# A two-layer attention kernel: the theta and phi copies move from SyncE's queue to ScalarE's, as four transfers in one slot

## The reference

```python
# layer 0, d = 64
t = W_theta x + b_theta; p = W_phi x + b_phi      # (n, 64, 1024)
f = softmax(t^T p / sqrt(64))                     # (n, 1024, 1024)
x = x + W_fuse (x f^T) + b_fuse
# layer 1
h = group_norm(x, 32 groups) * gn_w + gn_b
q, k, v = W_q h + b_q, W_k h + b_k, W_v h + b_v   # (n, 128, 1024)
a = softmax(q^T k / sqrt(128))
y = x + W_p (v a^T) + b_p
```

## Time and profile before

| | |
|---|---|
| median of the runs | 1922.38 us (1917.98 to 1924.8, 3 runs) |
| the profiled execution | 1909.72 us, span 1907.9 us |
| granted TensorE clock, mean | 0.978 |
| DMA engines' mean share | 81.3% |
| DMAs per kernel | 384 transposes, 256 copies from `tp_hl`, 128 + 128 for `rden`, 32 images in, 64 halves out |

### The profile page before, as it was taken

One profiled execution on the slowest core, in us unless ns is written; L12 is line 12 of the kernel. 1 busy time (PEld: TensorE's weight loads), 2 busy tenths in 40 slices (PEclk: granted clock), 3 DMA queues, 4 the chain that ended last, 5 costly groups with the idle time before them and its releaser, 6 DMA issues.

```text
span 1907.9 us, 34651 instructions
## 1 busy us (share of the span) xinstructions
PE 1715.2 (90%) x8970; PEld 1127.0 (59%) x8970; DVE 1359.3 (71%) x1541; ACT 1409.7 (74%) x2088; POOL 1381.1 (72%) x1449
## 2 busy tenths in 40 slices
PE   4698989999999999999989999999999999999986
PEld 3465655665656665665655655665656666655653
DVE  4577777777777777777777777777777777777764
ACT  3577777778777777877777877777877777877764
POOL 3567776778777778777778777678777778877754
PEclk9999999999999999999999999999999999999999
DMA  4688888888888888888887878888878988878874
GB/s 94 127 160 169 165 174 166 182 178 171 171 176 180 178 181 167 170 170 177 180 182 166 172 169 181 174 175 172 173 170 172 187 180 168 170 168 184 167 145 94
DMA packets 879542, 319.90 MB, mean 168 GB/s; under 512 B 825376, under 2 KB 826272, under 8 KB 879520
## 3 DMA queue, kind: packets, MB, share of 16 engines
q1 hardware_dynamic: 879520, 319.65, 81.3%
HBM read 50.86 MB, written 17.04 MB: 36 GB/s over the span
## 4 chain that ended last, share of the span: by engine, by line
PE 44%; SPq 20%; issue 12%; DMA 8%; POOL 5%; ACT 5%; DVE 4%; POOLq 0%; ACTq 0%; DVEq 0%
PE o_ps L448 17%; PE s_ps L448 16%; SPq L364 10%; PE m_ps L448 6%; DMA theta<-tp_hl 6%; PE s_ps L487 5%; SPq L426 2%; SPq L424 2%; SPq L427 2%; SPq L425 2%; DVE neg_max L750 2%; DMA rden_dram<-rden 1%; POOL k_lo L892 1%; DVE pair L767 1%; ACT e L649 1%
## 5 line engine op out<-in xcount | busy, mean ns | idle before, releaser
L750 DVE TENSOR_REDUCE neg_max<-s_ps 128x1 f32<-128x1024 f32 x512 | 625.5, 1222 | 233.3 <-PE s_ps L448 232.7
L448 PE MATMUL o_ps<-et,v_hi 128*128 128x512 f16 x2048 | 702.7, 385 | 57.5 <-issue 31.2
L448 PE MATMUL s_ps<-phi,theta 128*128 128x512 f32 x1024 | 334.5, 450 | 95.2 <-DMA theta<-tp_hl 86.2
L448 PE MATMUL o_ps<-et,v_lo 128*128 128x512 f16 x1024 | 393.4, 384 | 0.0
L448 PEld LDWEIGHTS o_ps<-et,v_hi 128*128 128x128 f16 x2048 | 204.8, 100 | 303.0 <-issue 98.2
L767 DVE SCALAR_TENSOR_TENSOR pair<-s_ps,pair 128x1024 f16<-128x1024 f32 x256 | 311.2, 1216 | 16.8 <-ACT pair L674 16.8
L649 ACT ACTIVATE s_ps<-s_ps,neg_max 128x1024 f32<-128x1024 f32 x256 | 277.3, 1083 | 58.9 <-DVE neg_max L750 58.3
L448 PEld LDWEIGHTS s_ps<-phi,theta 128*128 128x128 f32 x1024 | 197.2, 196 | 167.6 <-issue 102.4
L892 POOL TENSOR_TENSOR pair<-e_copied,pair 128x1024 f16<-128x1024 f32 x128 | 273.8, 2139 | 22.5 <-ACT pair L672 22.5
L761 DVE SCALAR_TENSOR_TENSOR et<-s_ps,et 128x1024 f16<-128x1024 f32 x128 | 156.8, 1225 | 175.4 <-ACT et L659 175.4
L674 ACT ACTIVATE pair<-s_ps 128x1024 f16<-128x1024 f32 x256 | 261.9, 1023 | 17.5
(11 more groups left out here) (130 smaller groups left out, 2873.0 us busy)
## 6 DMA issues: line engine op xcount, KB each, us to landing
phi<-tp_hl SPq DMA_DIRECT2D x128, 256.0 KB, 3.8
rden_row<-rden_dram SPq DMA_DIRECT2D x128, 256.0 KB, 3.8
xs<-in_x SPq DMA_DIRECT2D x32, 512.0 KB, 4.0
theta<-tp_hl SPq DMA_DIRECT2D x128, 128.0 KB, 3.8
out_y<-y_sb SPq DMA_DIRECT2D x64, 256.0 KB, 2.4
et<-pair SPq DMA_TRANSPOSE x384, 4.6
rden_dram<-rden SPq DMA_DIRECT2D x128, 2.0 KB, 2.1
w_f<-in_w_fuse_t SPq DMA_DIRECT2D x1, 64.0 KB, 2.3
```

Of the source, the lines that this page charges most:

```text
L448: mm = pe.matmul(out, lhs_t, rhs, start=start and n == 0, stop=stop and n == len(terms) - 1)
L750: nc.vector.tensor_reduce(neg_max[:, t % 4:t % 4 + 1], s_ps[:, part(t), :], AX.X, ALU.max, negate=True).then_inc(s_max, 1)
```

## The change

The copies leave SyncE. `tp_hl0` and `tp_hl1` become one tile `tp_hl` of two parts by 1024 pixels. ScalarE issues four transfers in slot 13, each for both halves, after `pair_hi` of tile 12 and after the wait for GpSimd's split of `tp1`. The reciprocals, on VectorE and on SyncE, are made, written and read back one slot earlier (`REC_LAG` = 5 in place of 6). The transpose of tile 12's pair is issued in slot 14; before, it was issued in slot 15 behind the one of tile 13. For the other copied tiles the slot stays.

```diff
+REC_LAG = 5
 LO_SLOTS = {0: 2, 4: 7, 8: 10, 12: 14}
+COPIED_OUT_SLOTS = {0: 3, 4: 8, 8: 11, 12: 14}
...
-TP_COPY_SLOTS = {12: "tp0", 14: "tp1"}
+TP_COPY_SLOT = 13
...
-        tp_hl = [sb(f"tp_hl{n}", [C, 2, HALF], F32R) for n in range(2)]
+        tp_hl = sb("tp_hl", [C, 2, N], F32R)
...
-                for t in [t for t in LO_SLOTS if LO_SLOTS[t] == s - 1]:
+                for t in [t for t in COPIED_OUT_SLOTS if COPIED_OUT_SLOTS[t] == s]:
                     move(it, t, copied_at, s_copied)
...
             def reciprocals_out(it, s):
-                first = s - 6
+                first = s - REC_LAG
...
             def reciprocals_in(it, s):
-                first = s - 7
+                first = s - REC_LAG - 1
...
-            def tp_copies(it, s):
-                unit = next((u for u, name in UNITS.items() if name == TP_COPY_SLOTS.get(s)), None)
...
-                    tp_copies(it, s)
...
+            def tp_copies(it, s):
+                if s != TP_COPY_SLOT or not here(mx_at, it, MX_SLOT):
+                    return
+                act.wait_ge(s_split, before(staged_at, it, s))
+
+                act.wait_ge(s_scores, before(tile_at, it, PHASE))
+                theta_hl, phi_hl = (tp_hl[rows, :, :].bitcast(F32) for rows in (slice(0, D), slice(D, C)))
+                act.dma_start(phi2[0:D, :, :].bitcast(F32), phi_hl).then_inc(s_tp_copy, 16)
+                act.dma_start(phi2[D:C, :, :].bitcast(F32), phi_hl).then_inc(s_tp_copy, 16)
+                act.dma_start(theta2[0:D, :].bitcast(F32), theta_hl[:, 0, :]).then_inc(s_tp_copy, 16)
+                act.dma_start(theta2[D:C, :].bitcast(F32), theta_hl[:, 1, :]).then_inc(s_tp_copy, 16)
...
                     inputs_hi(it, s)
+                    tp_copies(it, s)
...
             def reciprocals(it, s):
-                first = s - 6
+                first = s - REC_LAG
```

More of the change, by code:

```diff
@@ L59 @@
 X_MAX_SLOT = 7
+MX_SLOT = 9
 X_SLOT = 8
@@ L312, in attention_pair @@
         s_den = sem("den_scaled_ready")
-        s_tp_copy = [sem(f"theta_phi_copied{n}") for n in range(2)]
+        s_tp_copy = sem("theta_phi_copied")
         s_split_hi = sem("unit_split_hi")
@@ L463, in scores @@
                     if s == 0:
-                        for n in range(2):
-                            pe.wait_ge(s_tp_copy[n], 16 * TP_COPIES * before(mx_at, it, 0))
+                        pe.wait_ge(s_tp_copy, 16 * TP_COPIES * before(mx_at, it, 0))
                     if s == PHASE:
@@ L902, in split_units @@
                 if name[0] == "t":
-                    pool.wait_ge(s_tp_copy[half], 16 * TP_COPIES * or_none(before(mx_at, it, s) - 1))
-                    hi, lo = tp_hl[half][:, 0, :], tp_hl[half][:, 1, :]
+                    pool.wait_ge(s_tp_copy, 16 * TP_COPIES * or_none(before(mx_at, it, s) - 1))
+                    hi, lo = (tp_hl[:, n, half * HALF:(half + 1) * HALF] for n in range(2))
                     hi_read = hi.bitcast(F32)
```

## The result

The changed kernel is slower: 2016.96 us median (2008.17 to 2022.18, 4 runs) against 1921.56 us for the kernel before in the same runs (1917.98 to 1924.8, 4 runs). The ratio is 1.0491, 95% interval 1.0452 to 1.053. I had forecast 1896 us and a range up to 1952.

A forecast was written before the change was run, and what follows sets the result against it. The prediction took PE, busy 90% of 1907.9 us, to bound the kernel. Its terms, -48 + 22 + 0 = -26 us, gave 1884 us from the profiled execution, stated as 1896 us on the runs' median basis, range 1855 to 1952.

The forecast's parts named there:

- Waits for turned pairs: PE's value products in slots 2 and 6: earlier transposes remove most of 57.4 us of waits, 48 us gained.
- ScalarE's issue time: ScalarE in slot 13: four issues take 3.5 us a round and cost the kernel 0 us.
- the cover: Ahead of slot 0: ScalarE's delay of 3.2 us lies under PE's wait for the copies, 0 us.
- long issues: Rival: ScalarE's issues take 6.4 us, PE turns tile 15 2.1 us late, 1939 us; chance 0.06.
- Transposes beside the copies: Tile 12's transposes beside the last third of the copies delay them, +0.6 us a round between 0 and 2.6.
- the +0.7 of my sum: Landing of the copies before slot 0: the four terms together make it 0.7 us a round later, 22 us lost.
- the +3.7: Upper end of the copies' sum a round, whose lower end is -0.2; with all 2.6 us of tile 12's turn ahead.
- The rival of crowding: Rival: engines share turns evenly between copies and transposes, +2.4 us a round, 1948 us, or 1989 at +3.7; chance 0.20.
- the mixing: Copies and tile 12's transposes in flight together: 273 GB/s against 197, so their term was taken nearer to nothing.
- its two marks: Signs of a wrong main step: `theta` waits over 4.2 us a round, or last landing over 11 us after first issue.
- The hole between the two sets: Between the two sets of copies the DMA share is 0.37; one burst fills it, -0.6 us a round.
- gave away no head start: Start of the copies: the first half issued early gained nothing, as SyncE came to it only then; start term +0.4 us.

The follow-up runs named there:

- e2: The changed kernel with the reciprocals a slot later again (REC_LAG 6 in place of 5): 2013.59 us, ratio 1.0539 to the kernel before.
- e6: e1 with five extra activations of 128x1024 on ScalarE in slot 13, on a tile nothing else reads: 1953.29 us, ratio 1.0229 to the kernel before.
- e4: The changed kernel with tile 12's transpose on SyncE held until the copies have landed: 1980.29 us, ratio 1.0368 to the kernel before.
- e5: The changed kernel with tile 12's transpose on SyncE held until ScalarE has issued the fourth copy: 1986.34 us, ratio 1.0404 to the kernel before.
- e8: e1 with eleven throwaway products on PE in slot 0, ahead of the wait for the copies: 1877.85 us, ratio 0.984 to the kernel before.
- e1: The changed kernel with the four merged copies issued by SyncE, at the end of its slot 13: 1899.87 us, ratio 0.9957 to the kernel before.
- e11: The changed kernel with fourteen throwaway products on PE in slot 0, ahead of the wait for the copies: 1946.73 us, ratio 1.0198 to the kernel before.
- e7: The kernel before with the reciprocals a slot earlier and its second set of four copies in slot 13, not 14: 1836.76 us, ratio 0.9625.

## Why the prediction was wrong

- **Waits for turned pairs, 48 us gained: right.** They fell by 45 us. e2 shows that it takes the earlier reciprocals (55.6 us with the old lag), as I had argued.
- **ScalarE's issue time, 0 us: this step failed**, twice. The size: I took 3.5 us "since the number of instructions is the same"; it is 5.7, since the two `theta` copies over whole rows cost some 2 and 2.5 us. And the cover: I let the delay lie under PE's wait for the copies. e6 shows that ScalarE's time alone, with the copies unchanged, costs 53 us, where I had put 0. ScalarE's delay passes on to VectorE, whose wait for ScalarE's pair rose from 16.8 to 177.2 us (the groups below), and to PE's turn of tile 15 (3.8 us of waits before, 17.9 after). Of the rivals, long issues had this mechanism, with 0.06 and 1939 us. VectorE's rest of the pairs, its group on the page of the kernel before and then of the changed one:

```profile
L767 DVE SCALAR_TENSOR_TENSOR pair<-s_ps,pair 128x1024 f16<-128x1024 f32 x256 | 311.2, 1216 | 16.8 <-ACT pair L674 16.8
```

```profile
L765 DVE SCALAR_TENSOR_TENSOR pair<-s_ps,pair 128x1024 f16<-128x1024 f32 x256 | 312.1, 1219 | 178.4 <-ACT pair L659 177.2
```

- **Transposes beside the copies, +0.6 us a round: failed in 12 of 30 rounds.** In the short rounds PE waited 0.9 us longer than before (3.6 against 2.7 on average), near the +0.7 of my sum. In the long rounds it waited 4.0 to 6.4 us longer, which is over the +3.7 that I had bounded it with. My bound counted the bytes of tile 12's turn, 2.6 us. e4, e5 and e2 show the cause to be the start of the transposes ahead of the last copy's issue. The rival of crowding had the sign right and the size too small. I had put the mixing near nothing because of one microsecond at 273 GB/s; the long round's burst moved 162. In the words of the prediction, its two marks (over 4.2 us a round, over 11 us from issue to landing) were both passed.
- **PE's speed: left out.** No term of my sum was for the clock. 48.6 us of the loss are PE's busy time; e8 shows that filling the pause gives back 22 us in e1. In the changed kernel e11 gives back 56, part of it perhaps by fewer long rounds. A stall of 3 to 9 us in front of slot 0 was priced once and is paid twice.
- **The hole between the two sets, -0.6: right, and the smaller half of it.** The merged burst lands sooner (PE 9.5 us behind its start in e1, 10.2 before). But I had written that the first half "gave away no head start, since SyncE came to it only then". With the turns out earlier it comes to it sooner, and merging gives that away: e7 and e1 both issue on SyncE with the early reciprocals, and e7, with two sets, has 53.3 us of waits for `theta` against 103.7 and is 63 us faster. (They differ also in the place of tile 12's transpose, which no run changes alone.)
- **The range.** Its upper end of 1952 held crowding alone, or long issues alone, and no clock. The three came together.

By the two ratios, e1 stands 102 us under the changed kernel. e6 gives 53 of them to ScalarE's time. Keeping the transposes out gives back 17 to 24 (e4, e5). Between e5 and e6 lie 33 us, in the two profiles some 16 of PE's busy time, 13 of waits for `e` and 5 of waits for `theta`. e5's issues take some 0.2 us longer a round than e6's 5.41 of activations, and its `theta` comes 0.7 us later behind the burst's start (10.2 against 9.5). These may be the reason, but no run separates them, and I leave that split open.

The Trainium skill (DMA: Bandwidth & Descriptors, Issuing engines are not separate DMA queues) says that another engine saves only the time of issue, "which is usually small relative to the DMA itself". The first half agrees with these runs: a queue of its own brought the copies no sooner (PE 10.7 us or more behind the first issue in the 30 rounds of the changed kernel, against 9.5 with the same copies on SyncE in e1). The second half does not: 5.7 us of issue stand against 9.5 to 10.8 us from the first issue to PE's start, and a compute engine pays them.

## What to carry to other kernels

Before a DMA moves to another engine's queue, price the issue from a row of the same shape and put it on the new engine's timeline, with whoever waits for that engine; a compute engine with little idle time is no free place to issue from. When a read waits for the landing of a write on one queue, keep work that is needed anyway between the two. Two moves that each broke this order cost 3% here, and the two together, which kept it, won 3.8%; so an edit that moves one step of a queue is priced with the order that it leaves behind. And a stall of PE that lasts long enough to bring the granted clock down must be priced with the slower products behind it.

## What was new about the hardware

- Issue time goes neither by bytes nor by the number of transfers. The `phi` copy (64 x 2 x 1024, 512 KB) took 0.5 to 0.6 us to issue, the `theta` copy (64 x 1024, 256 KB) 1.9 to 2.6, on ScalarE and SyncE alike. In the kernel before, `phi` of 256 KB took 0.62 to 0.68 and the last `theta` of 128 KB 1.29. With no other row I can't say what sets it.
- Transposes of one queue that began 0.5 to 0.6 us before the end of the last issue on another queue went with a landing of that burst 3 to 5 us later; those that began 0.2 us after it did not (e5 and the two kinds of rounds). In the long round the DMA engines were full and moved 162 GB/s against 191.
- PE's granted clock fell to its lower level 27 times in the changed kernel between 200 and 1800 us, 208 us in all. With products in the pause ahead of slot 0 it fell 12 times (e11), and in e8 not once.
